# The down product of a feed-forward stage, turned so that its result comes out by tokens

## What is computed

```
x = x + 0.5 * moe(layernorm(x))        # 16 experts, top 4, and one shared expert
x = x + attention0(layernorm(x))
x = x + 0.5 * moe(layernorm(x))        # the same weights again
x = x + 0.5 * lut_ffn(layernorm(x))
x = x + attention1(layernorm(x))
x = x + 0.5 * lut_ffn(layernorm(x))

def moe(xt):                           # D = 256, E = 16, H = 128, HS = 512
    probs = softmax(xt @ w_router)
    top_w, top_i = top_k(probs, 4); top_w = top_w / sum(top_w); cw = scatter(top_w)
    g = silu(xt @ we1[e]) * (xt @ we3[e]) * cw[:, e]
    moe_out = sum over e of g @ we2[e]
    shared  = (silu(xt @ ws1) * (xt @ ws3)) @ ws2
    return shared / 5 + moe_out * 4 / 5

def lut_ffn(x):                        # inner width 688, every weight one of 16 table values
    return (silu(x @ lut[gate_idx].T) * (x @ lut[up_idx].T)) @ lut[down_idx].T
```

## Time and profile before

| | us |
|---|---|
| median of 3 runs | 2749.64 (2746.08 to 2749.93) |
| the profiled execution, whole | 2749.25 |
| its span, first to last instruction | 2747.5 |
| routing stages | about 0 to 230, and 1170 to 1400 |
| table stages | about 1630 to 1890, and 2500 to 2742 |

### The profile page before, as it was taken

How to read it: one execution, slowest core, us unless ns; L and a number is a source line. 1 busy time by engine, 2 the same in 40 slices (tenths; PEclk the granted TensorE clock), 3 DMA queues, 4 the chain that set the end, 5 groups by cost and what they waited for, 6 DMA issues and landing times. The chain is left out here.

```text
span 2747.5 us, 50426 instructions
## 1 busy us (share of the span) xinstructions
PE 2430.6 (88%) x15174; PEld 1583.9 (58%) x15190; DVE 1973.1 (72%) x5616; ACT 1474.8 (54%) x3654; POOL 939.3 (34%) x1304
## 2 busy tenths in 40 slices
PE   6996997898999999959969967996889999996998
PEld 4776995565233333547759956775633333345776
DVE  5885887776888887658858856764678888864544
ACT  3443663343578787624436633343637877773343
POOL 4774664112232232237746641110122232220000
PEclk8998998999799999979989988998879999998999
DMA  4546555565435455355465552322544455434010
GB/s 144 178 168 178 185 184 185 199 219 164 93 77 116 93 111 111 95 166 175 169 171 186 185 201 105 101 92 81 169 96 101 99 102 119 95 81 150 31 39 23
DMA packets 256413, 359.75 MB, mean 131 GB/s; under 512 B 43494, under 2 KB 205591, under 8 KB 250007
## 3 DMA queue, kind: packets, MB, share of 16 engines
q1 hardware_dynamic: 220822, 249.53, 34.9%
q0 software_dynamic: 35328, 106.99, 10.5%
HBM read 199.16 MB, written 156.47 MB: 129 GB/s over the span
## 5 line engine op out<-in xcount | busy, mean ns | idle before, releaser
L1299 DVE CUSTOM_DVE_ANT_0 attn_heads_masked_s<-attn_heads_s_ps,attn_heads_causal 128x768 bf16<-128x768 f32 (+7 forms) x1024 | 726.6, 754 | 137.2 <-PE attn_heads_s_ps L1101 121.6
L1218 ACT ACTIVATE attn_heads_probs<-attn_heads_st_ps 128x512 f32<-128x512 f32 (+3 forms) x1536 | 663.4, 494 | 227.5 <-PE attn_heads_st_ps L1120 213.6
L2123 POOL DMA_INDIRECT y_dram<-moe_expert_y_sb,moe_expert_rows_y x288 | 277.0, 962 | 187.9 <-ACT moe_expert_rows_y L2211 131.9
L1136 PE MATMUL attn_heads_o_ps<-attn_heads_probs,attn_v_sb 128*32 128x512 f32 (+3 forms) x3072 | 328.6, 500 | 0.6 <-POOL attn_heads_probs L1043 0.4
L1616 POOL DMA_INDIRECT xs_dram<-moe_route_xn,rows_at x256 | 263.9, 1031 | 96.9 <-issue 75.0
L1043 POOL TENSOR_SCALAR_AFFINE_SELECT attn_heads_probs<-attn_heads_probs 128x512 f32<-128x512 f32 x256 | 163.5, 638 | 360.3 <-ACT attn_heads_probs L1218 355.0
L1120 PE MATMUL attn_heads_st_ps<-attn_heads_more_st 99*128 99x512 bf16 x960 | 261.2, 329 | 0.1
L1101 PE MATMUL attn_heads_s_ps<-attn_heads_more_st 96*128 96x512 bf16 (+1 forms) x960 | 245.9, 334 | 8.0 <-DVE attn_heads_row_max L1299 4.3
L1120 PEld LDWEIGHTS attn_heads_st_ps<-attn_heads_more_st 99*128 99x128 bf16 x960 | 84.4, 97 | 212.2 <-ACT attn_heads_probs L1218 158.4
L2151 PE MATMUL moe_expert_gu_ps<-moe_w_hi,moe_expert_xT_hi 128*128 x576 | 189.0, 328 | 1.7 <-DVE moe_expert_xT_lo L2234 1.7
L2193 ACT ACTIVATE moe_expert_xT_hi<-moe_expert_xT_ps 128x256 fp32r<-128x256 f32 x288 | 110.9, 385 | 131.4 <-PE moe_expert_xT_ps L2137 130.4
(11 more groups left out here) (277 smaller groups left out, 6097.6 us busy)
## 6 DMA issues: line engine op xcount, KB each, us to landing
moe_expert_x_sb<-xs_dram SPq DMA_DIRECT2D x288, 136.0 KB
attn_stack<-y_dram POOLq DMA_DIRECT2D x32, 512.0 KB, 5.5
o_dram<-attn_heads_oT SPq DMA_DIRECT2D x64, 256.0 KB, 3.7
lut_y_sb<-y_dram POOLq DMA_DIRECT2D x32, 512.0 KB, 5.8
moe_route_w_raw<-in_L_ffn_we_dram SPq DMA_DIRECT2D x96, 128.0 KB, 3.7
q_dram<-attn_proj_parts SPq DMA_DIRECT2D x32, 384.0 KB, 4.1
k_dram<-attn_proj_parts SPq DMA_DIRECT2D x32, 384.0 KB, 3.1
x_mid<-moe_route_x_sb SPq DMA_DIRECT2D x16, 512.0 KB, 2.9
```

The source lines that it names most:

```text
L1136: last = pe.matmul(o_ps[h * VW:(h + 1) * VW, use % OB, TILE - w:TILE], v_sb[:, at:at + VW], probs[:, G % NR, h, 0:w], start=(j == 0), stop ...
L1218: act.activation(probs[:, G % NR, h, 0:w], st_ps[:, v % NB, 0:w], ACT.Exp, scale=scale)\
L1299: dve.tensor_tensor_reduce(out=masked_s[:, use % 4, 0:w], in0=s_banks[:, at * TILE:at * TILE + w], in1=causal[:, SEQ - w:SEQ], scale=1.0, ...
L2123: pool.indirect_dma_start(y_dram, bass.IndirectOffsetOnAxis(rows_y[:, s % RI:s % RI + 1], 0), y_sb[:, s % AHEAD, :], None)\
```

## The change

`down` is turned in both functions. A block of 128 tokens of the hidden chunk is now the stationary operand, and the 256 columns of the down weights are the moving one, so that y comes out by tokens, as x lies in SBUF. `y_ps` has the same two banks, now as 4 blocks of 128 tokens by 256 features. Per chunk it is 12 matmuls of 256 columns in place of 6 of 512. The eight that need only the high half of the hidden chunk are issued first, and wait for that half alone; the four with the low half follow, behind a wait of their own.

`yT`, `copy_y` and `y_turn` are gone. `add_y` adds from `y_ps` straight into x, both halves one behind the other, in chunk 1 of the next tile. It waits for the tile's last `down`. A new semaphore `y_free` counts the adds: `down` of chunk 0 waits for both adds of the tile before (it waited for the two copies), and the store of x waits for them too. `t_ps` has only the input's transposes as users, so `turns_of_tiles` is gone.

The core of the diff for the routing stage:

```diff
-        y_ps = ps("y_ps", [P, KD, TILE])
+        y_ps = ps("y_ps", [P, SUB, D])
...
                 def down(g):
                     t, c = divmod(g, NC)
-                    pe.wait_ge(h_ready, g + 1)
+                    pe.wait_ge(hh_ready, g + 1)
                     if c == 0 and t > 0:
-                        pe.wait_ge(y0_free, t)
-                        pe.wait_ge(y1_free, t)
-                    for m in range(KD):
-                        cols = slice(2 * D + m * P, 2 * D + (m + 1) * P)
-                        last = chain(y_ps[:, m, :], [(s_hi[:, c, cols], h_hi[:, g % HB, :]), (s_hi[:, c, cols], h_lo[:, g % HB, :]),
-                                                     (s_lo[:, c, cols], h_hi[:, g % HB, :])], c == 0, c == NC - 1)
+                        pe.wait_ge(y_free, 2 * t)
+                    for low in range(2):
+                        if low:
+                            pe.wait_ge(h_ready, g + 1)
+                        for s in range(SUB):
+                            toks = slice(s * P, (s + 1) * P)
+                            pairs = [(h_lo, s_hi)] if low else [(h_hi, s_hi), (h_hi, s_lo)]
+                            for n, (h, w) in enumerate(pairs):
+                                last = pe.matmul(y_ps[:, s, :], h[:, g % HB, toks], w[:, c, 2 * D:3 * D],
+                                                 start=(c == 0 and not low and n == 0 and s % 2 == 0), stop=(c == NC - 1 and low == 1),
+                                                 skip_group_check=True)
                     last.then_inc(h_used, 1)
...
-                        if c >= 2 and t > 0:
-                            y_turn(t - 1, c - 2)
...
-                def copy_y(n):
+                def add_y(n, half):
                     dve.wait_ge(h_used, (n + 1) * NC)
-                    if n > 0:
-                        dve.wait_ge(t_full, TURN["y", n - 1, 1] + 1)
-                    dve.tensor_copy(yT[:, 1, :], y_ps[:, 1, :]).then_inc(y1_free, 1)
-
-                def add_y(n, half):
-                    dve.wait_ge(t_full, TURN["y", n, half] + 1)
                     xs = x_sb[:, n % RX, 2 * half:2 * half + 2, :]
-                    dve.tensor_tensor(xs, xs, t_ps[:, :].rearrange("p (s d) -> p s d", d=D), ALU.add).then_inc(t_free, 1)
+                    dve.tensor_tensor(xs, xs, y_ps[:, 2 * half:2 * half + 2, :], ALU.add).then_inc(y_free, 1)
...
                         if g >= 1:
                             hidden_lo(g - 1)
-                        if c == 1 and t > 0:
-                            copy_y(t - 1)
                         if c < 2 and t + 1 < TILES:
                             x_lo(t + 1, c)
                         if c == 1 and t > 0:
                             locate(t)
...
-                        if c >= 2 and t > 0:
-                            add_y(t - 1, c - 2)
+                        if c == 1 and t > 0:
+                            add_y(t - 1, 0)
+                            add_y(t - 1, 1)
```

More of the change, by code:

```diff
@@ L80 @@
 POS_TOP = float(1 << 17)
-def turns_of_tiles(inputs_first):
-    order = [("x", 0, 0), ("x", 0, 1)]
-    for t in range(TILES):
-        ahead = [("x", t + 1, 0), ("x", t + 1, 1)] if t + 1 < TILES else []
-        behind = [("y", t - 1, 0), ("y", t - 1, 1)] if t > 0 else []
-        order += ahead + behind if inputs_first else behind + ahead
-    order += [("y", TILES - 1, 0), ("y", TILES - 1, 1)]
-    return {key: n for n, key in enumerate(order)}
 def load_rows_y(pool, u, y_sb, y_used, y_loaded, y_dram):
@@ L1755, in _ @@
                 down(TILES * NC - 1)
-                for half in range(2):
-                    y_turn(TILES - 1, half)
             @block.scalar
@@ L2454, in down @@
                     rows = rows_of(c)
-                    pe.wait_ge(h_ready, g + 1)
+                    pe.wait_ge(hh_ready, g + 1)
                     if c == 0 and t > 0:
-                        pe.wait_ge(y0_free, t)
-                        pe.wait_ge(y1_free, t)
-                    for m in range(KD):
-                        cols = slice(2 * D + m * P, 2 * D + (m + 1) * P)
-                        last = chain(y_ps[:, m, :], [(w_hi[rows, c, cols], h_hi[rows, g % HB, :]), (w_hi[rows, c, cols], h_lo[rows, g % HB, :]),
-                                                     (w_lo[rows, c, cols], h_hi[rows, g % HB, :])], c == 0, c == NC - 1)
-                    last.then_inc(h_used, 1)
-                def y_turn(n, half):
-                    if half == 0:
-                        pe.wait_ge(y0_free, n + 1)
-                        pe.wait_ge(y1_free, n + 1)
-                    pe.wait_ge(t_free, TURN["y", n, half])
-                    for s in range(2):
-                        for m in range(KD):
-                            last = pe.transpose(t_ps[:, s * D + m * P:s * D + (m + 1) * P],
-                                                yT[:, m, (2 * half + s) * P:(2 * half + s + 1) * P], ident[:, :])
-                    last.then_inc(t_full, 1)
+                        pe.wait_ge(y_free, 2 * t)
+                    for low in range(2):
+                        if low:
+                            pe.wait_ge(h_ready, g + 1)
+                        for s in range(SUB):
+                            toks = slice(s * P, (s + 1) * P)
+                            pairs = [(h_lo, w_hi)] if low else [(h_hi, w_hi), (h_hi, w_lo)]
+                            for n, (h, w) in enumerate(pairs):
+                                last = pe.matmul(y_ps[:, s, :], h[rows, g % HB, toks], w[rows, c, 2 * D:3 * D],
+                                                 start=(c == 0 and not low and n == 0 and s % 2 == 0), stop=(c == NC - 1 and low == 1),
+                                                 skip_group_check=True)
+                    last.then_inc(h_used, 1)
                 x_turn(0, 0)
@@ L2483, in _ @@
                             down(g - 2)
-                        if 2 <= c < 4 and t > 0:
-                            y_turn(t - 1, c - 2)
                         if c >= 4 and t + 1 < TILES:
```

63 lines of the change are left out of this document (13 added, 50 removed).

## The result

| | us |
|---|---|
| before, median of 4 runs beside it | 2749.78 (2746.08 to 2750.59) |
| the changed kernel, median of 4 runs | 2787.11 (2782.56 to 2794.62) |
| ratio, 95% interval | 1.0144 (1.0128 to 1.0159) |
| the changed kernel's profiled execution, whole | 2789.05 |
| its span | 2787.0 |

The forecast was 2767 us and a range up to 2781. The sign was right, the size was not: +37 us where the sum said +17.5. The time is near that of rival C (2785).

What follows compares the result with a forecast made beforehand. GpSimd's 22.5 us loop was taken to bound the routing stages, TensorE the table stages. 2749.25 - 14.8 (table) + 33.0 (routing, where TensorE becomes the bound) = 2767.5, stated as 2767 us, range 2750 to 2781.

Steps and rivals of the forecast that it cites:

- the sum: Whole kernel: 2749.25 us, less 14.8 in the table stages, plus 33.0 in the routing stages, giving 2767.5.
- rival C: Routing stages: two half-clock stretches behind each wait, or dearer 256-column matmuls; 2785 us, chance 0.07.
- the one half-clock stretch that lies nearest: Routing stage: a 3.4 us stretch costing 1.54 us, assumed behind nearly all five long waits, +7.2 us per stage.

Runs made afterwards that it cites:

- e4: Kernel before with the change made in the table stage alone: 2733.17 us against 2748.99, ratio 0.9936.
- e14: Kernel before with the change in the table stage alone, on the third chip: 2908.43 us against 2927.07, ratio 0.9937.
- e12: Changed kernel, routing adds ahead of x_lo, 9 wide matmuls ahead of the wait for normalised rows: 2726.28 us against the kernel before's 2746.82, ratio 0.9918.
- e10: Changed kernel with 7 unused 512-column matmuls ahead of each routing wait for the y bank: 2749.84 us against the kernel before's 2746.82, ratio 1.0012.
- e3: Changed kernel with 14 unused 512-column matmuls ahead of each routing wait for the y bank: 2752.26 us against the kernel before's 2748.99, ratio 1.0007.
- e9: Changed kernel with the next tile's router logits issued ahead of the wait for the y bank: 2743.32 us against the kernel before's 2746.82, ratio 0.9979.
- e2: Changed kernel with the routing stage's two adds between locate and find_moments: 2757.03 us against the kernel before's 2748.99, ratio 1.0031.
- e15: Changed kernel with the routing stage's adds ahead of x_lo, on the third chip: 2932.87 us against the kernel before's 2927.07, ratio 1.0020.

## What to carry to other kernels

When an operand moves out of a copy and into the instruction that uses it, the buffer's release moves to that instruction's place in the consumer's queue: put it where the copy stood. A new wait on TensorE is to be priced with the clock behind it, and not from the one half-clock stretch that lies nearest: ask also what runs behind the wait. Here 16 matmuls of 32 columns there made the stretches longer. To find out what a wait costs apart from the clock, fill it with matmuls whose result nobody reads; if they make the kernel faster, the clock was the larger part.

Of the versions here the table stage alone is the one to keep: 0.6% under before on the two chips on which it ran (e4, e14). The turned product in the routing stage, with the adds early, adds nothing to that which a measurement shows on the first (e12, on the second, stands 0.2 points lower, with intervals that overlap), and loses 0.8% on the third.

## What the runs showed of the hardware

- Filling an idle TensorE with wide matmuls made the kernel 35 us faster (2787.1 to 2752.3) though it computes more; with half as many it stood as close to before (e10 3.0 us over it, e3 3.3).
- Half-clock stretches behind equal waits of 4.05 us were 3.4 to 13.7 us long. Behind equal waits of 2.35 us, in those cases that had one, they were 3.4 us in nine of ten with wide matmuls following (e9; the tenth 6.8) and 6.8 to 10.2 us in all nine with 32-column matmuls following (e2). In e10, with 2.32 us and the 32-column matmuls, eight of ten waits had none.
- A third chip runs the kernel before in 2927 us for 2749 on the first, and the changed versions traced there have pauses of up to 2 us between TensorE's instructions (e15). What a version gains changes with the chip: adds early is 0.6% faster than before on the first and level with it on the third.
